# Zeros in front of the expert queues, a later wait for constants, and 67 matmuls without a reader

## The reference

```
x = _layernorm(x + _L0_attn_ref(x))                      # dilated attention, 16 heads of 16, segments of 64
x = _layernorm(x + _L0_xattn_ref(x, ctx_512, Wq, Wkv, Wout))   # causal cross attention to a context of width 64
x = _layernorm(x + _L0_ffn_ref(x, gate_w, w_gate, w_up, w_down))
```

## Time and profile before

| what | value |
|---|---|
| median of 3 runs | 602.8 us (600.79 to 603.04) |
| the profiled execution | 603.31 us; its span 601.6 us |
| PE busy | 510.0 us (85%) |
| POOL, DVE, ACT busy | 399.8, 373.3, 337.0 us |
| DMA | 121.30 MB, mean 202 GB/s |
| mean granted TensorE clock | 0.935 of 2.4 GHz |

### The profile page before, as it was taken

The page is one execution under the profiler, slowest core; times in us unless marked ns, Lnnn a source line. Parts: engine busy times, 40 slices in busy tenths (PEclk is TensorE's granted clock), DMA queues, the critical chain, the costliest instruction groups (busy, mean ns, idle before and its releaser), DMA issues.

```text
span 601.6 us, 17385 instructions
## 1 busy us (share of the span) xinstructions
PE 510.0 (85%) x5065; PEld 391.7 (65%) x5066; DVE 373.3 (62%) x1527; ACT 337.0 (56%) x1204; POOL 399.8 (66%) x604
## 2 busy tenths in 40 slices
PE   2689999999999999961099999999999999994894
PEld 2456556556665666531078888888888888883773
DVE  1368988888888888843025555555555555552665
ACT  2266767677777777740036666666666666660112
POOL 5653766667777776677327777777777778774743
PEclk9599999999999999975569999999999999996998
DMA  9999999962222222226846655665566555657994
GB/s 200 281 243 288 333 339 341 336 236 87 92 88 93 87 87 90 92 107 233 281 147 182 188 174 176 188 186 178 171 189 185 182 166 181 188 169 282 425 418 154
DMA packets 82302, 121.30 MB, mean 202 GB/s; under 512 B 13012, under 2 KB 71902, under 8 KB 80225
## 3 DMA queue, kind: packets, MB, share of 16 engines
q1 hardware_dynamic: 64896, 79.51, 43.3%
q0 software_dynamic: 14016, 38.44, 18.0%
q10 hardware_dynamic: 3360, 2.98, 1.5%
HBM read 56.07 MB, written 69.01 MB: 208 GB/s over the span
## 4 chain that ended last, share of the span: by engine, by line
PE 60%; issue 10%; POOL 10%; DMA 6%; DVE 6%; ACT 4%; ACTq 3%; SPq 1%; POOLq 0%; DVEq 0%
PE bank L793 17%; PE bank L809 11%; PE bank L785 7%; PE bank L607 5%; POOL queues L533 5%; DMA wall<-results 4%; PE bank L803 3%; PE bank L617 3%; PE bank L625 2%; ACT pr L870 2%; ACTq L297 2%; PE bank L706 2%; PE bank L646 2%; PE bank L661 1%; PE bank L601 1%
## 5 line engine op out<-in xcount | busy, mean ns | idle before, releaser
L559 POOL DMA_INDIRECT results<-ys,wcol x152 | 150.2, 988 | 26.2 <-POOL pscrap L548 24.1
L533 POOL DMA_INDIRECT queues<-x,xidx x128 | 130.0, 1016 | 35.5 <-issue 35.2
L793 PE MATMUL bank<-wall,xtT 128*128 x616 | 128.3, 332 | 0.1
L870 ACT ACTIVATE pr<-bank,nmax 128x128 f32<-128x128 f32 x256 | 91.1, 377 | 17.5 <-DVE nmax L1022 15.2
L793 PEld LDWEIGHTS bank<-wall,xtT 128*128 128x128 f32 x616 | 99.7, 196 | 0.5 <-issue 0.5
L963 ACT ACTIVATE ys<-bank,wcol 128x256 f32<-128x256 f32 x152 | 72.1, 474 | 45.1 <-PE bank L809 44.8
L1216 DVE SCALAR_TENSOR_TENSOR tg<-th,bank 128x96 f32<-128x96 f32 x154 | 39.2, 254 | 90.8 <-ACT th L957 90.0
L785 PE MATMUL bank<-ident,xt 128*128 128x128 f32 x310 | 63.8, 288 | 35.5 <-DMA xt<-queues 23.8
L785 PEld LDWEIGHTS bank<-ident,xt 128*128 128x128 f32 x310 | 59.2, 198 | 50.2 <-DMA xt<-queues 24.8
L809 PE MATMUL bank<-wall,hT 96*128 x304 | 91.3, 381 | 0.0
L607 PE MATMUL bank<-kP,qS 128*128 128x512 f32 x128 | 67.8, 611 | 5.7 <-DVE eAT L1062 5.7
(11 more groups left out here) (178 smaller groups left out, 872.6 us busy)
## 6 DMA issues: line engine op xcount, KB each, us to landing
xt<-queues SPq DMA_DIRECT2D x162, 160.0 KB, 2.2
results<-zeros SPq DMA_DIRECT2D x16, 1024.0 KB
wall<-results SPq DMA_DIRECT2D x16, 1024.0 KB, 13.7
queues<-zeros SPq DMA_DIRECT2D x32, 160.0 KB, 4.0
wall<-in_L_ffn_w_gate SPq DMA_DIRECT2D x4, 768.0 KB, 11.2
wall<-in_L_ffn_w_up SPq DMA_DIRECT2D x4, 768.0 KB, 13.2
wall<-in_L_ffn_w_down SPq DMA_DIRECT2D x4, 768.0 KB, 12.6
results<-ys,wcol POOLq DMA_INDIRECT x152, 2.6
```

The source lines that it names most:

```text
L533: pool.indirect_dma_start(xg, bass.IndirectOffsetOnAxis(ap=xidx[:, par, k:k + 1], axis=0), x2[:, par, :], None, bounds_check=last_row, oob ...
L559: pool.indirect_dma_start(yr, bass.IndirectOffsetOnAxis(ap=wcol[:, u, 1:2], axis=0), ys[:, u, :], None, bounds_check=last_y, oob_is_err=Fa ...
L793: ins = pe.matmul(bank[2 + u % 2][:, 0:2 * INTER].rearrange("p (g i) -> p g i", g=2), xtT[:, u % 2, kk, :], wall[:, bass.ds(e, GU)].rearrange(
L870: ins = act.activation(pr[:, g % 2, q, :], pS[g % 2][:, q * P:(q + 1) * P], ACT.Exp, bias=nmax[:, 4 * g + q:4 * g + q + 1], accum_out=den[ ...
```

## The change

`queues` gets 128 rows more. A token's row moves up by 128 (`eoff_i`, base P), so that each expert's first 128 rows stay free, and these rows are filled with zeros by 4 DMAs of 8 experts each on SP's queue, between the idle zeros and the zeros of `results`. The blocks of an expert now end with its last token; its first block begins as many rows before the first token as the blocks lack. The row of a block is computed with two more table products (`lackb` with `past` and `begun`), `tab_p` and the pads after the tables are gone. PE's wait for B_CONST moves from before step 0 into it, ahead of the first product of scores; and PE does 67 mask products into the bank pS[0] that nothing reads: 14, 2 and 5 before waits of step 17, 4, 3 and 3 before waits of the tables, 36 after the tables' last wait.

```
-PADS = (14, 28)
+PADS = 4
...
+            heads = xg[0:NE * STRIDE, :].rearrange("(e s) w -> s e w", s=STRIDE)
+            for k in range(PADS):
+                n = NE // PADS
+                sp.dma_start(heads[0:P, n * k:n * (k + 1), :],
+                             zeros[:, :].unsqueeze(1).to_broadcast([P, n, XW])).then_inc(pad_zero, 16)
...
-            sp.wait_ge(dveH.sem, dveH.at(0, "tp"))
-            pad_queues(sp, ET.SP, 0, PADS[0], pad_zero)
...
-            sp.wait_ge(pad_zero, 16 * PADS[1])
-            sp.wait_ge(pad_late, 16 * (NE - PADS[1]))
+            sp.wait_ge(pad_zero, 16 * PADS)
...
-                put(pool.iota, eoff_i[:, :], [[STRIDE, NE]], base=0, channel_multiplier=0)
+                put(pool.iota, eoff_i[:, :], [[STRIDE, NE]], base=P, channel_multiplier=0)
...
-            pool.wait_ge(dveH.sem, dveH.at(0, "tp"))
-            pad_queues(pool, ET.Pool, PADS[1], NE, pad_late)
...
+            def idle_products(n):
+                for _ in range(n):
+                    pe.matmul(pS[0][:, :], identb[:, :], causal[:, :].unsqueeze(1).to_broadcast([P, 4, P]),
+                              start=True, stop=True)
...
+                    if ends:
+                        idle_products(14)
                     pe.wait_ge(dveN.sem, dveN.at(r + 2, "x2"))
...
+                    if isinstance(a, int) and a == 0:
+                        pe.wait_ge(consts, B_CONST)
                     pe.wait_ge(dveK, a + 1)
...
             small_weights()
-            pe.wait_ge(consts, B_CONST)
...
-                pe.wait_ge(dveH.sem, dveH.at(0, "skipb"))
+                idle_products(3)
+                pe.wait_ge(dveH.sem, dveH.at(0, "nblkb"))
...
+                idle_products(3)
                 pe.wait_ge(dveH.sem, dveH.at(0, "n"))
                 pe.matmul(pW[0:1, 140:140 + TAB], onesb[0:NE, 0:1], past[:, :], start=True, stop=True)
-                pe.matmul(pW[0:1, 326:326 + TAB], skipb[:, :], past[:, :], start=True, stop=True
+                pe.matmul(pW[0:1, 326:326 + TAB], skipb[:, :], past[:, :], start=True, stop=False)
+                pe.matmul(pW[0:1, 326:326 + TAB], lackb[:, 0:1], past[:, :], start=False, stop=False)
+                pe.matmul(pW[0:1, 326:326 + TAB], lackb[:, 1:2], begun[:, :], start=False, stop=True
...
+            idle_products(36)
             pe.wait_ge(experts_loaded, 16 * 3 * (NE // 8))
...
-            act.wait_ge(dveH.sem, dveH.at(0, "tp"))
-            pad_queues(act, ET.Activation, PADS[0], PADS[1], pad_zero)
...
-                dve.tensor_tensor(tab_p[0:1, :], pW[0:1, 96:96 + NE], eoff[0:1, :], ALU.add).then_inc(s, 1)
...
+                dve.scalar_tensor_tensor(lackb[:, 0:1], nblk[:, :], float(P), took[:, :], ALU.mult, ALU.subtract
+                                         ).then_inc(s, 1)
+                dve.scalar_tensor_tensor(lackb[:, 1:2], nblk[:, :], -float(P), took[:, :], ALU.mult, ALU.add
+                                         ).then_inc(s, 1)
...
+                dve.tensor_scalar(begun[:, :], blk[:, :], nblk[:, 0:1], cum[:, 0:1], ALU.add, ALU.is_ge).then_inc(s, 1)
```

More of the change, by code:

```diff
@@ L33 @@
 IDLE = 2 * UN + 2
-XG_ROWS = NE * STRIDE + IDLE * P
+XG_ROWS = NE * STRIDE + (1 + IDLE) * P
 Y_ROWS = NB * P * TOPK
@@ L46 @@
 B_CONST = FIRST_CONST + 23
-N_CONST = 54
+N_CONST = 53
 assert MAXB % UN == 0
@@ L187, in build @@
         past = sb("past", [NE, TAB], BF16)
+        begun = sb("begun", [NE, TAB], BF16)
+        lackb = sb("lackb", [NE, 2], BF16)
         tjunk = sb("tjunk", [1, MAXB // UN])
@@ L192, in build @@
         tab_x = sb("tab_x", [1, TAB + 2 * LEAD], I32)
-        tab_p = sb("tab_p", [1, NE], I32)
         tab_n = sb("tab_n", [1, 1], I32)
@@ L237, in build @@
         peH = Steps(sem("peH"), "count place table")
-        dveH = Steps(sem("dveH"), "took tp nblk nblkb skipb cum past n n2 fe fx tg tw tx")
+        dveH = Steps(sem("dveH"), "took nblk nblkb skipb lack over cum past begun n n2 fe fx tg tw tx")
         peF = {n: sem(f"peF_{n}") for n in ("xT", "gu", "hT", "y")}
@@ L291, in neighbours @@
                 skip_runtime_bounds_check_because="the tables hold rows and columns of these arrays only")[1]
[L293 to L297, removed]
         def store(eng, b):
@@ L648, in front @@
                 ins.then_inc(peA.sem, 1)
+            def idle_products(n):
+                for _ in range(n):
+                    pe.matmul(pS[0][:, :], identb[:, :], causal[:, :].unsqueeze(1).to_broadcast([P, 4, P]),
+                              start=True, stop=True)
             def step(a, b, r, par):
                 pb = 1 - par
+                ends = a is None and b is None
                 if b is not None:
@@ L684, in step @@
                         pe.wait_ge(dveA.sem, dveA.at(a, "scale"))
+                    if ends:
+                        idle_products(2)
                     pe.wait_ge(actX.sem, actX.at(r + 2, "r"))
@@ L711, in step @@
                 if r is not None:
+                    if ends:
+                        idle_products(5)
                     pe.wait_ge(dveR.sem, dveR.at(r, "pickb"))
@@ L750, in _ @@
             small_weights()
-            pe.wait_ge(consts, B_CONST)
             def tables():
+                idle_products(4)
                 pe.wait_ge(dveR.sem, dveR.at(NB - 1, "seen"))
                 pe.wait_ge(actB.sem, actB.at(NB - 1, "T3"))
-                pe.matmul(pW[0:1, 96:96 + NE], onesb[:, 0:1], seen[:, :], start=True, stop=True)
                 pe.matmul(pW[0:NE, NE:NE + 1], seen[:, :], onesb[:, 0:1], start=True, stop=True
                           ).then_inc(peH.sem, 1)
-                pe.wait_ge(dveH.sem, dveH.at(0, "skipb"))
+                idle_products(3)
+                pe.wait_ge(dveH.sem, dveH.at(0, "nblkb"))
                 pe.matmul(pW[0:NE, NE + 1:NE + 2], upto[:, :], nblkb[:, :], start=True, stop=True)
@@ L1188, in tables @@
                                   ).then_inc(s, 1)
-                dve.tensor_tensor(tab_f[0:1, 1, :], pW[0:1, 326:326 + TAB], blk[0:1, :], ALU.add).then_inc(s, 1)
+                dve.scalar_tensor_tensor(tab_f[0:1, 1, :], blk[0:1, :], float(P), pW[0:1, 326:326 + TAB],
+                                         ALU.mult, ALU.add).then_inc(s, 1)
                 dve.wait_ge(s, H("fe"))
@@ L1194, in tables @@
                 dve.wait_ge(s, H("fx"))
-                dve.tensor_scalar(tab_x[0:1, LEAD:LEAD + TAB], tab_f[0:1, 1, :], float(P), None, ALU.mult
+                dve.tensor_scalar(tab_x[0:1, LEAD:LEAD + TAB], tab_f[0:1, 1, :], float(P), None, ALU.add
                                   ).then_inc(s, 1)
```

7 lines of the change are left out of this document (2 added, 5 removed).

## The result

The changed kernel takes 591.9 us (median of 4 runs, 591.3 to 593.2); the kernel before took 602.3 beside it. The ratio is 0.983, with a 95% interval from 0.981 to 0.986. The forecast was 591.5, in a range from 587.0 to 596.5. The profiled execution of the changed kernel has a span of 591.0 us, 10.6 less than that of before (601.6).

The account below looks back on a forecast made before the run. The end of the pads was taken to bound the stage before the expert loop, scatters next; -10.0 + 0.7 - 1.5 - 0.5 = -11.3 us gave 592.0 against the profiled execution, 591.5 against the median, range 587.0 to 596.5.

Parts of the forecast that it names:

- The pads, -10.0: Between tables and expert loop: with the pads moved, the first block load goes at 289.0 instead of 299.05, -10.0 us.
- the bound of -9.5: Pads' gain before the first load if the last scatter lands in 2.6 us, the page's median, instead of 2.1.
- POOL's stall: POOL's 1.93 us wait ahead of the next to last tile's scatter; kept, up to -1.6 us more if gone.
- The zeros under the front, +0.7: Front: moved pads add 17.8 us of zeros, 1.2 steps at 0.58 us each; +0.7 us, bounds 0 and 0.9.
- The late wait, -1.5: Front's start: L661 no longer waits for POOL's constants, and the gain passes to the last scatter; -1.5 us (0 to -1.9).
- Products: End of front and tables: mask products at 0.22 us each are hidden in PE's waits; taken as 0.
- Rivals 3 and 4: Mask products cost 0.32 us each (593.9 us, chance 0.07) or 0.54 us each, making PE late (609 us, chance 0.03).
- The clock at the loop's start, -0.5: Expert loop's start: the clock falls again around the first block, so only -0.5 us of 3.6 is taken.
- the 3.6 us that were called possible: Expert loop's start: gain set for a high clock, from at most 4.3 us, as PE also waits there.
- rival 1: The clock holds into the expert loop, giving the other 3.1 us: 588.4 us; chance 0.25.
- Rival 2: The front gives its gain back: pads delay scatters, the start's 1.5 us is lost; 594.1 us, chance 0.13.
- rival 2's sign: Before the expert loop: a first block load after 291 would show that the front gave its gain back.

Follow-up runs that it names:

- The pads alone: Changed kernel without its 67 unused products and with the constants wait back at its old place: 592.6 us, 0.985 of the kernel before.
- the nine profiles: Profiles of kernels with the four pads written once and without the 22 extra transposes; first-to-last-step stretch 221.1 to 223.1 us, on average 222.04.
- The two other profiles: The changed kernel run twice more with no edit: 591.1 and 592.1 us, both 0.983 of the kernel before.
- the longer bridge: Changed kernel with 42 products, not 36, after the last wait and register load before the loop: 590.4 us; with 8 more in the loop's start, 590.4 twice.
- the warm start: Changed kernel plus 22 unused identity transposes in PE's first waits: 594.0 us; with 42 products before the loop and 8 in its start as well, 591.1.

## Why the prediction was right

*The pads, -10.0.* Right in kind and size. The bound of the stage was the last pad, and the scatters were next in line, as said; but the last pad was one of ACT's, issued at 296.19 and landed at 298.75, not one of SP's, on which the prediction looked for what filled the gap. The register loads that it priced at 4.7 us from SP's queue took some 2.3 in the changed kernel: the table was written at 277.70, and SP stood at L351 from 280.0 on (287.8 less the 7.8 that it waited). Neither bears on the sum, since the scatters end later. The load came 2.72 us behind the last scatter's start, not 2.1. The landing, 2.50, was nearer to the median of the page, 2.6, than to the one taken from the end of the kernel. That makes -9.40, the bound of -9.5 and not the value. The pads alone measured -9.5 in the medians.

*POOL's stall.* It was kept in the sum, and stayed.

*The zeros under the front, +0.7.* Right in the place where it was looked for. SP issued its zeros for 18.6 us longer (88.7 us from the first idle pad to the last result zero, 70.1 before; 17.8 forecast), and the sixth and seventh steps, which they newly cover (the sixth in part), are 0.7 us longer together in the nine profiles, 0.9 in the first. What makes it, one more wait for a scatter a step, was not in the prediction. The whole stretch grew by more, about 1.5 on average and 2.04 in the first profile, where the clock fell in the third step (16.99 us against 15.49); the prediction had no term for that, and the 0.3 in the last step is not explained.

*The late wait, -1.5.* Right in kind, somewhat too large in the profiles: 1.05 and 1.42 us between profiles with the same kind of rise, and 1.04 at L661 itself, once the 0.31 of the earlier start is taken off; 1.5, with an interval from 0 to 3.0, by the ratio of the kernel that has it alone. The 3.4 us that the two profiles show at the first step contain some 2 us of a rise at another time, which is no part of the change.

*Products.* Hidden, as said, but for some 1 us at L678 that the scatters cover: 31 of them in PE's waits, the table's last write at 277.47 in time for the scatters. Four products in a row took 1.02 us and a single one 0.38, so at 2.4 GHz they stand (1.02 - 0.38) / 3 = 0.21 apart. The 36 behind the table took 9.60 us and not 7.7, as the clock was at 1.2 GHz from some 277.7 to 281.1 (0.93 in 276 to 278, 0.72 in 276 to 280, 0.86 in 280 to 284), behind the 1.36 us in which PE waited for the table. Rivals 3 and 4, which needed 0.32 and 0.54, fell; the rule of the Trainium skill (TensorE: Matmul & The Clock Gate, Part 3, "The mechanism"), by which these weight loads could not overlap, does not hold for them.

*The clock at the loop's start, -0.5.* Right that it falls around the first block, wrong that some of its return is kept: in the first profile it was back at about 301.6, as long after the first load as before, and the stretch behind the load was 0.4 longer. The two other profiles were 1.4 to 1.8 us shorter there than before, so -0.5 is within what single profiles show. Of the 3.6 us that were called possible, the versions with the longer bridge got about 3 behind the load in their profiles (299.2 to 299.5 against 302.5 before); against the changed kernel their runs are 1.6 shorter. So what rival 1 needs can be had; the change as it stands did not reach it.

*Rival 2* did not come in the first profile, where the last scatter is 1.64 us earlier, but that profile had its early rise to help. In the two others, with a late rise like that of before, the last scatter starts at 286.41 and 287.59, 0.5 earlier and 0.7 later than before: there the front gave the start's gain back, or nearly. The first load (289.12 and 290.31) still stays short of the 291 that the prediction named as rival 2's sign.

The forecast was met to 0.4 us, the sum less closely: -11.3 against -10.6 in the span and -10.4 between the medians. In the two profiles the pads brought 0.6 less than forecast, the expert loop 0.9 less, and the front 0.8 more (1.64 against 1.5 - 0.7). The last is luck: an early rise, no part of the change, gave some 2 us, and without it the front would have brought nothing. So the pads are predicted, and the closeness of the rest is partly chance.

## What to carry to other kernels

A transfer that needs no result of the stage before it, but stands behind it in a queue, is worth moving for the whole distance to the next thing in line: find that next thing first, with the landing of its last DMA, and the gain is a difference of two rows. Zeros under busy work were cheap here but not free: each step that they newly covered took 0.7 to 0.9 us more, which the average of steps under zeros had priced (0.58), and a wait for a small transfer's landing is where it shows. Work that only kept a clock up paid when it reached up to the first real work behind the wait: a bridge that ended 2.0 to 2.9 us early gained nothing that could be measured, and one that reached the first block, in two of its three measurements with 8 products more behind it, gained 1.6 us. And a single profile of each kernel is a thin base: two kinds of rise in the first 30 us moved the end of its first step by 2.55 us, more than either of the two smaller parts of this change is worth.

## What the runs showed of the hardware that was not expected

- The time of TensorE's rise in the first 30 us differs between runs of one kernel, some 22 to 23.5 or 27.5 to 29 us, and moves the end of the first step by 2.55 us. 22 more transposes before it did not settle it; what does stays open.
- The granted clock reads 1.00 in the first 26 us of several profiles where the durations are those of 1.2 GHz (L600 at 23.90 in 1.92 us, windows 1.00). In that stretch durations say more than the clock's column. The first matmuls of the warm start show it as well: the 13 from 2.30 us on stand (3.04 - 0.42) / 12 = 0.22 us apart, as the six at 15.78 do ((1.54 - 0.42) / 5 = 0.22), while four transposes at 29.07 of the same profile, behind the rise, took 0.60 us together.
- The granted clock fell behind a wait of 1.09 us in the middle of the front (0.50 in the window behind it), and the step took 1.5 us more than that of before. A wait of 1.08 us in the same place of the second and the third profile left it at 1.00.
